# First attention of a four-stage kernel: reciprocals spread by DMA through DRAM, four banks of scores

## The reference, cut to what is needed

```python
b, s, x = input.shape                      # 8, 512, 128
w = qkv * (3.0 * x * h * n) ** (-0.25)
q, k, v = jnp.einsum('bsx,xAnh->Abnsh', input, w)
q = q + q_bias[:, None, :]
a = jnp.einsum('bnqh,bnkh->bnqk', q, k) * h ** (-0.5)
...
a = a + relative_causal(pos_scores)
a = jax.nn.softmax(jnp.where(mask, a, NEG_INF), axis=-1)
o = jnp.einsum('bnqk,bnkh->bqnh', a, v).reshape(b, s, n * h)
out = o @ (out_kernel * (fan_in * fan_out) ** (-0.25)) + out_bias
```

## Time and profile before

| what | us |
|---|---|
| median of 3 runs | 1664.89 (1663.42 to 1665.79) |
| the profiled execution | 1676.82 |
| its span, first to last instruction | 1675.1 |
| first attention, in the span | some 40 to 799 |
| TensorE matmuls busy, over the span | 1421.9 (85%) |
| VectorE busy | 1262.4 (75%) |
| ScalarE busy | 971.0 (58%) |
| GpSimd busy | 879.9 (53%) |
| mean granted TensorE clock | 0.948 |

### The profile page before, as it was taken

One profiled execution on the slowest core, in us unless ns is written; L12 is line 12 of the kernel. 1 busy time (PEld: TensorE's weight loads), 2 busy tenths in 40 slices (PEclk: granted clock), 3 DMA queues, 4 the chain that ended last, 5 costly groups with the idle time before them and its releaser, 6 DMA issues. The chain is left out here.

```text
span 1675.1 us, 38178 instructions
## 1 busy us (share of the span) xinstructions
PE 1421.9 (85%) x12519; PEld 834.2 (50%) x12519; DVE 1262.4 (75%) x2722; ACT 971.0 (58%) x1921; POOL 879.9 (53%) x1203
## 2 busy tenths in 40 slices
PE   4899989898998999897589887489899899898736
PEld 3566666666666666665356555123333333332216
DVE  3788888887888888886688888377787787777534
ACT  2677767676776767675244443156666666665431
POOL 2877778777787777775445555211221221222524
PEclk9899999999999999999699999599999999999977
DMA  5645545454454545544000000411011011010001
GB/s 160 123 113 127 123 98 125 97 122 110 110 125 105 114 111 118 116 110 94 0 2 0 0 0 0 146 48 35 27 39 36 26 39 36 26 40 28 13 12 27
DMA packets 372881, 116.47 MB, mean 70 GB/s; under 512 B 341675, under 2 KB 369312, under 8 KB 372704
## 3 DMA queue, kind: packets, MB, share of 16 engines
q1 hardware_dynamic: 369472, 111.36, 27.9%
q10 hardware_dynamic: 1824, 3.15, 0.6%
q0 software_dynamic: 1536, 1.34, 0.3%
HBM read 20.36 MB, written 12.89 MB: 20 GB/s over the span
## 5 line engine op out<-in xcount | busy, mean ns | idle before, releaser
L541 ACT ACTIVATE prob<-score_ps,nmax 128x512 f32<-128x512 f32 (+3 forms) x512 | 264.9, 526 | 209.0 <-DVE nmax L594 209.0
L1563 DVE TENSOR_REDUCE a_nm<-a_s 128x1 f16<-128x512 f32 x512 | 324.8, 687 | 55.5 <-PE a_s L1335 53.6
L1489 ACT ACTIVATE a_pt<-a_st 128x1024 f32<-128x1024 f32 x256 | 260.4, 1021 | 131.4 <-PE a_st L1353 116.3
L130 POOL TENSOR_TENSOR gate<-mhalf 128x1 f32<-128x1 f32 (+1 forms) x284 | 124.2, 437 | 259.3 <-ACT k L566 137.6
L1335 PE MATMUL a_s<-a_kop,a_qop 128*128 128x512 f16 x512 | 199.6, 391 | 64.2 <-DVE a_nm L1563 47.4
L606 DVE SCALAR_TENSOR_TENSOR p<-prob,p 128x1280 f16<-128x1280 f32 x128 | 204.6, 1598 | 49.8 <-ACT p L550 49.8
L594 DVE TENSOR_REDUCE nmax<-score_ps 128x1 f32<-128x512 f32 (+3 forms) x512 | 213.0, 475 | 3.4 <-PE score_ps L455 3.3
L452 PE MATMUL score_ps<-k_h,q_h 128*128 128x512 f16 (+3 forms) x512 | 158.2, 309 | 22.4 <-ACT prob L541 14.2
L550 ACT ACTIVATE p<-prob 128x1280 f16<-128x1280 f32 x128 | 163.8, 1279 | 6.5
L888 ACT ACTIVATE hid<-fps,b_cols 128x512 f32<-128x512 f32 x130 | 86.3, 687 | 127.2 <-PE fps L848 127.2
L694 POOL TENSOR_TENSOR q_l<-q,q_h 128x512 f16<-128x512 f32 x130 | 152.9, 1176 | 10.8
(11 more groups left out here) (331 smaller groups left out, 3433.5 us busy)
## 6 DMA issues: line engine op xcount, KB each, us to landing
a_qop<-q_parts SPq DMA_DIRECT2D x32, 128.0 KB
a_kop<-k_parts SPq DMA_DIRECT2D x128, 24.0 KB
x_tok<-in_L_attn_input_dram SPq DMA_DIRECT2D x4, 512.0 KB, 12.3
pt<-p SPq DMA_TRANSPOSE x128, 4.1
e_w<-in_L_ffn_w_dram SPq DMA_DIRECT2D x1, 2048.0 KB, 8.3
q_parts<-a_q_h SPq DMA_DIRECT2D x16, 128.0 KB
k_parts<-a_k_h SPq DMA_DIRECT2D x16, 128.0 KB
out_dram<-a_res SPq DMA_DIRECT2D x8, 256.0 KB
```

The lines of the kernel that those rows point to most:

```text
L541: ins = nc.scalar.activation(prob[h][:, P_OFF[c]:P_OFF[c] + w], score_ps[u][:, col:col + w], ACT.Exp, bias=nmax[h][:, c:c + 1], accum_out= ...
L1489: nc.scalar.activation(pt[kc % 2][r][:, :, :], st_ps[r][:, :, :], ACT.Exp, scale=1.0 / SC).then_inc(exp_done[r], 1)
L1563: nc.vector.tensor_reduce(nm[g % 2][:, c, hh:hh + 1], s_ps[c % 2][:, :], AX.X, ALU.max, negate=True).then_inc(max_done[c % 2], 1)
```

## The change

- The matmuls into `r_ps` and `r_copy` go. SyncE stores the reciprocals of each head, [128 partitions, 4], as 512 numbers in DRAM (`store_r`, behind that head's transpose) and reads them back to 64 partitions a head (`spread_r`, both heads, one pair later, behind the next transpose). `normalise` waits for `pv_mm` and for these reads and reads the reciprocals as they lie in DRAM, query by query with the four chunks inside, so at a step of four f32.
- `score_ps` has four banks; `bank(h, k, u)` deals them in turn to the six units of a pair. A unit waits for the exponentials of the unit four before it.
- In VectorE's stream reciprocals(0) stands before low(0); `batch_stats`, and GpSimd's inverse deviation, move from p = 7 to p = 2. `batch_norm` stays at p = 7.
- In the second stage two semaphores are made one.

```diff
-        r_sb = sb("r_sb", [P, S], F32)
+        r_bc = [sb(f"r_bc{k}", [P, S], F32) for k in range(2)]
...
+        rsum = [[sb(f"rsum{h}{k}", [P, QC], F32) for k in range(2)] for h in range(2)]
+        r_dram = nc.dram_tensor("r_parts", (2, 2, P * QC), F32).ap()
...
+        score_ps = [ps(f"score_ps{u}") for u in range(4)]
+        q_ps, kv_ps, pv_ps, out_ps = ps("q_ps"), ps("kv_ps"), ps("pv_ps"), ps("out_ps")
+        bank = lambda h, k, u: score_ps[(2 * k + 3 * h + u) % 4]
...
+            def store_r(h, n, k):
+
+                sp.wait_ge(r_done[h], n + 1)
+                sp.sem_inc(turn_open, 1)
+                if later(n, 2):
+                    sp.wait_ge(r_in, 32 * (n - 1))
+                    sp.sem_inc(turn_open, 1)
+                sp.dma_start(r_dram[k, h].rearrange("(q c) -> q c", c=QC), rsum[h][k][:, :]).then_inc(r_stored, 16)
+
+            def spread_r(n, k):
+
+                sp.wait_ge(r_stored, 32 * (n + 1))
+                sp.sem_inc(turn_open, 1)
+                if later(n, 2):
+                    sp.wait_ge(o_done, n - 1)
+                    sp.sem_inc(turn_open, 1)
+                for h in range(2):
+                    sp.dma_start(r_bc[k][64 * h:64 * h + 64, :], r_dram[k, h:h + 1, :].broadcast_to([64, P * QC])).then_inc(r_in, 16)
+
             def body(n, t, b, p, k):
                 if later(n, 1):
                     turn(1, n - 1, 1 - k)
+                    store_r(1, n - 1, 1 - k)
                 turn(0, n, k)
+                if later(n, 1):
+                    spread_r(n - 1, 1 - k)
+                store_r(0, n, k)
...
-                    if h == 1 or later(n, 1):
-                        pe.wait_ge(exp_done[1 - h], count(n + h - 1, u))
+                    if u > 0 and (h == 1 or later(n, 1)):
+                        pe.wait_ge(exp_done[1 - h], count(n + h - 1, u - 1))
+                    if u == 0 and later(n, 1):
+                        pe.wait_ge(exp_done[h], count(n - 1, 2))
...
-                pe.wait_ge(r_done[1], n + 1)
                 if later(n, 1):
                     pe.wait_ge(o_done, n)
-                for c in range(QC):
-                    for h in range(2):
-                        nc.tensor.matmul(r_ps[64 * h:64 * h + 64, c * P:(c + 1) * P], rsum[k][:, c, h:h + 1].to_broadcast([P, 64]),
-                                         m.ident[:, :], start=True, stop=True)
...
-                if later(n, 2):
-                    r_copy(n - 2)
...
-            def normalise(n):
-                dve.wait_ge(r_out, n + 1)
+            def normalise(n, k):
+                dve.wait_ge(pv_mm, n + 1)
+                dve.wait_ge(r_in, 32 * (n + 1))
                 if later(n, 1):
                     dve.wait_ge(out_mm, n)
-                nc.vector.tensor_tensor(o32[:, :], pv_ps[:, :], r_sb[:, :], ALU.mult).then_inc(o_done, 1)
+                nc.vector.tensor_tensor(o32[:, :].rearrange("p (c q) -> p c q", q=P), pv_ps[:, :].rearrange("p (c q) -> p c q", q=P),
+                                        r_bc[k][:, :].rearrange("p (q c) -> p c q", c=QC), ALU.mult).then_inc(o_done, 1)
...
-                if behind:
+                if at(p, 2) and not at(b, 0):
                     batch_stats(b - 1)
+                reciprocals(0, n, k)
                 low(0, n, k)
                 if later(n, 2):
-                    normalise(n - 2)
-                reciprocals(0, n, k)
-                maxima(1, n)
+                    normalise(n - 2, k)
+                maxima(1, n, k)
...
-                if at(p, PAIRS - 1) and not at(b, 0):
+                if at(p, 2) and not at(b, 0):
                     layer_norm_gpsimd(nc, pool, m, b - 1, mv, ve, rstd)
```

More of the change, by code:

```diff
@@ L323, in rel_attention_phase @@
         turned = [pair(f"turned{h}") for h in range(2)]
-        pv_mm, r_out, o_done, out_mm, y_done = sem("pv_mm"), sem("r_out"), sem("o_done"), sem("out_mm"), sem("y_done")
+        pv_mm, o_done, out_mm, y_done = sem("pv_mm"), sem("o_done"), sem("out_mm"), sem("y_done")
+        r_stored, r_in = sem("r_stored"), sem("r_in")
         pool_steps, turn_open = sem("ra_pool"), sem("turn_open")
@@ L408, in body, with last @@
                     turn(1, n - 1, 1 - k)
+                    store_r(1, n - 1, 1 - k)
                 turn(0, n, k)
-            schedule(sp, lambda: None, body, lambda: turn(1, B * PAIRS - 1, 1))
+                if later(n, 1):
+                    spread_r(n - 1, 1 - k)
+                store_r(0, n, k)
+            def last():
+                n = B * PAIRS
+                turn(1, n - 1, 1)
+                store_r(1, n - 1, 1)
+                spread_r(n - 1, 1)
+            schedule(sp, lambda: None, body, last)
             sp.wait_ge(m.f0_loaded, m.F0_LOADS)
@@ L440, in project_v, with scores @@
                 mm.then_inc(v_mm, 1)
-            def scores(h, n):
+            def scores(h, n, k):
                 pe.wait_ge(q_split[h], n + 1)
@@ L445, in scores @@
                 for u in range(3):
-                    if h == 1 or later(n, 1):
-                        pe.wait_ge(exp_done[1 - h], count(n + h - 1, u))
+                    if u > 0 and (h == 1 or later(n, 1)):
+                        pe.wait_ge(exp_done[1 - h], count(n + h - 1, u - 1))
+                    if u == 0 and later(n, 1):
+                        pe.wait_ge(exp_done[h], count(n - 1, 2))
                     for c, col in UNIT_CHUNKS[u]:
                         w = P * (c + 1)
-                        o, qs = score_ps[u][:, col:col + w], slice(c * P, (c + 1) * P)
+                        o, qs = bank(h, k, u)[:, col:col + w], slice(c * P, (c + 1) * P)
                         nc.tensor.matmul(o, q_h[h][:, qs], m.k_h[h][:, 0:w], start=True, stop=False)
@@ L503, in body @@
                 bx, pw = (b + 1, 0) if at(p, PAIRS - 1) else (b, p + 1)
-                scores(0, n)
+                scores(0, n, k)
                 if later(n, 1):
@@ L513, in body @@
                     weighted_values(n - 2, t - 1, k)
-                scores(1, n)
+                scores(1, n, k)
                 pe.wait_ge(q_out[0], n + 2)
@@ L540, in exps @@
                         w = P * (c + 1)
-                        ins = nc.scalar.activation(prob[h][:, P_OFF[c]:P_OFF[c] + w], score_ps[u][:, col:col + w], ACT.Exp,
+                        ins = nc.scalar.activation(prob[h][:, P_OFF[c]:P_OFF[c] + w], bank(h, k, u)[:, col:col + w], ACT.Exp,
                                                    bias=nmax[h][:, c:c + 1], accum_out=sums[h][:, c:c + 1])
@@ L568, in body, with maxima @@
             def body(n, t, b, p, k):
-                exps(0, n, [0, 1])
+                exps(0, n, k, [0, 1])
                 k_copy(n + 1)
-                exps(0, n, [2])
+                exps(0, n, k, [2])
                 high(0, n, t, k)
-                if later(n, 2):
-                    r_copy(n - 2)
-                exps(1, n, [0, 1, 2])
+                exps(1, n, k, [0, 1, 2])
                 v_high(n, k)
                 high(1, n, t, k)
[L579 to L583, removed]
             nc.scalar.preload_act_table(ACT.Exp)
-            schedule(act, lambda: k_copy(0), body, last)
+            schedule(act, lambda: k_copy(0), body, lambda: None)
         @block.vector
         def _(dve):
-            def maxima(h, n):
+            def maxima(h, n, k):
                 for u in range(3):
@@ L593, in maxima @@
                     for c, col in UNIT_CHUNKS[u]:
-                        ins = nc.vector.tensor_reduce(nmax[h][:, c:c + 1], score_ps[u][:, col:col + P * (c + 1)],
+                        ins = nc.vector.tensor_reduce(nmax[h][:, c:c + 1], bank(h, k, u)[:, col:col + P * (c + 1)],
                                                       AX.X, ALU.max, negate=True)
@@ L600, in reciprocals @@
                 if later(n, 2):
-                    dve.wait_ge(pv_mm, n - 1)
-                nc.vector.reciprocal(rsum[k][:, :, h], sums[h][:, :]).then_inc(r_done[h], 1)
+                    dve.wait_ge(r_stored, 32 * (n - 1))
+                nc.vector.reciprocal(rsum[h][k][:, :], sums[h][:, :]).then_inc(r_done[h], 1)
             def low(h, n, k):
@@ L648, in body @@
                 pw = 0 if wrap else p + 1
-                maxima(0, n)
+                maxima(0, n, k)
                 if at(p, 2) and not at(b, 0):
@@ L678, in last @@
                 low(1, n - 1, 1)
-                normalise(n - 2)
-                normalise(n - 1)
+                normalise(n - 2, 0)
+                normalise(n - 1, 1)
                 batch_sum(B - 1)
@@ L1004, in _ @@
             for raw, hi, lo in matrices:
-                nc.gpsimd.tensor_copy(hi, raw).then_inc(aw_split, 1)
-            pool.wait_ge(aw_split, 5)
+                nc.gpsimd.tensor_copy(hi, raw).then_inc(w_split, 1)
+            pool.wait_ge(w_split, 4 + 5)
             for raw, hi, lo in matrices:
```

10 lines of the change are left out of this document (2 added, 8 removed).

## The result

The changed kernel takes 1673.08 us (median of 7 runs, 1670.04 to 1675.78), the kernel before 1665.27 on the same chip (7 runs, 1663.42 to 1665.79): a ratio of 1.0049, 95% interval 1.0037 to 1.006, or 8 us slower. Forecast were 1673.3 and the same sign. The sum behind the number holds in the loop of the first attention, with errors in its terms that partly cancel. Two things that it lacks, some +4 us at the start of the phase and -4.5 us in later stages, happen to cancel as well: that part is luck.

The account below looks back on a forecast made before the run. No engine was full; a chain between VectorE and ScalarE was taken to set the 11.02 us pair. Terms -4.6 - 16.1 + 2.1 + 26.5 + 0.5 = +8.4 from the 1664.89 us median gave 1673.3, range 1645 to 1693.

Parts of the forecast that it names:

- The chain: In each pair, VectorE and ScalarE waiting on each other set its length: 11.02 us before, 11.36 after.
- The stepped read: In normalise, reading r at a step of four words costs 0.42 us in each of 63 pairs: +26.5 us.
- Reciprocals(0): On VectorE, moving it ahead of low(0) hides its 0.08 us in idle time in 57 pairs: -4.6 us.
- The wait for rstd: At batch_norm, end of pair 7, VectorE's 2.3 us wait for GpSimd goes in 7 batches: -16.1 us.
- Statistics at p = 2: Layer norm's statistics on VectorE, moved from p = 7, make that pair 0.3 us longer, 7 times: +2.1 us.
- Matmuls, `r_copy`, four banks: On TensorE and ScalarE, removing the first two and adding a score bank gains nothing, being off the chain: 0.
- The DMAs: On SP's queue, r's stores and spreads land 2.7 us before normalise wants them: 0.
- The end: At the last normalise, r_copy's 0.6 us goes but the last r arrives by store and spread: +0.5 us (-0.6 to +3).
- The free read: Rival: in normalise the strided read costs nothing, -18.1 us, 1646.8 us; chance 0.18.
- The granted clock: Rival: TensorE, idling about 2 us a pair, drops to its lower clock: +8 us on the forecast, 1681; chance 0.05.
- r landed 2.8 us behind its issue: Rival: store and spread take over 2.7 us more than allowed, so normalise waits: 1735 us at 1 us; chance 0.03.
- TensorE wasn't on the chain: Rival judged here: removing r's matmuls takes TensorE's 0.85 us off each pair, 1620 us; chance 0.02.

Follow-up runs that it names:

- e2: The kernel before with only the normalising multiply's read of the reciprocals at a step of 4 elements: ratio 1.0143 to the kernel before, +23.8 us.
- e8: The kernel before with the 16 matmuls that spread the reciprocals issued twice in each pair: 1662.0 us, ratio 0.9983 to the kernel before.
- e11: The changed kernel with 33 lone 128x512 f32 multiplies added behind the last batch, at various steps: 0.69 us at two words, 1.05 at four in SBUF.
- e3: The kernel before with only VectorE's new order: reciprocals(0) ahead of low(0), statistics and GpSimd's rstd at p = 2: ratio 0.9963 to the kernel before.
- e12: e5 with the multiply's step moved from SBUF to PSUM and TensorE loading weights at a step of 4: ratio 0.9902 to the kernel before.
- e5: The changed kernel with third-stage weight loads issued later and p = 7's four batch_norm steps moved behind maxima(0): 1656.9 us, ratio 0.9961 to the kernel before.
- e9: e5 with the normalising multiply moved into VectorE's wait for v_h, output projection, residual bias and batch sum moved too: ratio 0.981 to the kernel before.

## Why the prediction was right, and where it wasn't

- **The chain.** Right: it put the pair at 11.36 us, and it is 11.34. e2's price is paid in full in the regular pairs, and e8's 0.85 us of TensorE in none.
- **The stepped read**, +26.5: 0.376 x 63 = +23.7. The value taken from GpSimd's copy (0.42) was 12% too high; the estimate by the Trainium skill's "Vector Engine (DVE) Microarchitecture Reference", section 5.2, was nearer (0.35). The bounds held. What was missing was that a step of two words would have been free (0.69 us in e11); that section's rule of two adjacent words would have charged for it.
- **Reciprocals(0)**, -4.6: 0.06 in most pairs of e3, and 0.06 in after's regular pair (0.38 - 0.32), so -3.4.
- **The wait for rstd**, -16.1: the wait went, and 0.55 us a batch of it came back. Beyond the 0.32 of every pair the wrap gained 1.75, -12.2 in all. The prediction named GpSimd's q_l and bounded this at 4 us (it is 3.9), but left it out of its sum. In e3 it took back 1.8 of the 2.3, more than that bound. So the weak step of the prediction is the belief that 0.63, read off one pair, bounds it: in after it held by the place at which the two engines happened to meet.
- **Statistics at p = 2**, +2.1: +0.7. `low`(0) fell from 2.17 to 1.46 there, by 0.71 where 0.63 was reckoned; that leaves 0.19, and the pair shows 0.10.
- **Matmuls, `r_copy`, four banks**, 0: right in this order of work, taken together; no run has the four banks alone. e3's 35 us of VectorE waiting for pv show that with the matmuls in place the new order brings another wait, hidden by the one for p.
- **The DMAs**, 0: right in the loop, where `normalise` never waited for one; wrong at the start. SyncE's queue was reckoned in a regular pair only, and the 24 loads ahead of the first transpose were not counted: +4.
- **The end**, +0.5: +0.1 to +0.3.
- **Not in the sum at all**: some -4.5 in later stages, of which some 2 go with an earlier return of TensorE's clock in the third stage. Without it the time would have been about 1677.5.
- **Rivals.** The free read is refuted by e2. The granted clock was 1.00 in the pair shown, and 0.953 over the profiled execution against 0.948 in before's. r landed 2.8 us behind its issue, and TensorE wasn't on the chain.

So the number is better than the working, and its closeness (0.2 us) is luck. The four terms of the loop were put at +7.9 and came to +8.0 to +8.5 in the traces (+8.8 by the sizes above), with errors of -2.8, +1.2, +3.9 and -1.4 in them. The start of the phase (+4) and the later stages (-4.5) were not in the sum, and cancelled.

## What to carry to other kernels

Find the chain first: work taken off an engine with slack is worth nothing, and 0.38 us put on the chain costs 24. If a layout must hold a step somewhere, put it on VectorE's PSUM source or keep it to 8 bytes in SBUF; don't buy it off with a DMA of 4-byte pieces. Better still, put the instruction where its engine waits anyway. When a wait is taken away, ask what the other engine will be doing at the moment to which the work behind it moves, and move it on until it stands beside an idle GpSimd or in front of another wait.

## What the runs showed of the hardware

- A 128x512 f32 multiply on VectorE: 0.69 us flat, at 8 bytes' step and with PSUM stepped; 1.00 to 1.07 us at 16 to 512 bytes in an SBUF source, 1.06 at 16 in the output (e11).
- TensorE's f32 weight load of 128 columns: 192 ns flat (after), 330 at a step of 16 bytes (e12).
- An f32 tensor_scalar of 128x128 took 0.33 us, or 1.18 when GpSimd's tensor_tensor had begun 0.5 us before it. `low` takes 1.46 us, and 2.31 begun 0.2 us behind one. GpSimd's subtraction took 2.45 us instead of 1.16 begun 0.03 us behind a `low` (e5). The cause is read from the timelines and from e5, which moved the instruction; no run took GpSimd away.
- A store of 512 pieces of 4 bytes, twice in 19 us, doubled the landing time of transposes on its queue (4.1 to 9.1 us).
- The third stage changed by 2.6 us when matmuls were added to the first. In the faster profiles TensorE's granted clock rose about 4 us sooner in that stage and fell for about 3 us less near its end. The same stage took 543 to 546 or 557 to 560 us on different chips, with 12 us of waits credited to "remote" in the traces of the slower sort that were looked at (before, e9).
